# Cross-attention and a quantised FFN in one program: weights quantised in the loop, first rows fed through while the attention drains

## The chip, the cores and the metric

One Trainium2 chip, one core of it. The time is the device time of one execution in microseconds (us), and less is better. The core has engines that run side by side, each through its own list of instructions: TensorE (PE; its weight loads are shown apart as PEld), VectorE (DVE), ScalarE (ACT), GpSimd (POOL) and SyncE (SP), which here issues all DMAs. They wait for each other by semaphores alone.

## What is computed

The kernel takes `x` (8 batches x 112 rows x 512) and a context (8 x 375 x 256), and computes a cross-attention of 16 heads of 128 columns with RMS norms on q and k, and behind it an FFN of 512 -> 2048 -> 512 whose matmuls work on values rounded to 8 bits. Cut to what matters:

```
def rmsnorm(x, g): return x * rsqrt(mean(square(x), -1) + 1e-5) * g
h = layernorm(x)
q, k, v = h @ Wq, ctx @ Wk, ctx @ Wv            # 16 heads of 128
attn = softmax(rmsnorm(q, gq) @ rmsnorm(k, gk).T / sqrt(128))
x = x + (attn @ v) @ Wo
# FFN
X1 = layernorm(x)
X1_q = round(X1 * (127 / max|X1| of the row));    W1_q = round(W1 * (127 / max|W1|))
X2 = gelu(X1_q @ W1_q.T * (sX1 * sW1 / 127**2) + B1)
X2_q = round(X2 * (127 / max|X2| of the row));    W2_q = round(W2 * (127 / max|W2|))
x = x + X2_q @ W2_q.T * (sX2 * sW2 / 127**2) + B2
```

One scale holds for a whole weight matrix, so it is known only when all of that matrix has been read.

## The kernel before

**Attention.** Every operand of a matmul is kept as two float32r tensors, a high part and the rest (`_hi`, `_lo`), and each product is three matmuls. The work is cut into NI = 16 iterations `it`: 8 groups of two heads for the first four batches, then the same 8 for the last four. Each iteration has NB = 4 batch steps b; t = 4 * it + b numbers them from 0 to 63. A batch step computes K (`k_projection`), its squares and their sums (`k_norm`), scores, maximum, exponential, the transposes of the probabilities and their product with the context (`prob_ctx`). It is spread over several steps: in step t an engine works on t, t-1, t-2 and t-3 at a time. Once per iteration come `q_projection` (24 matmuls), `q_norms`, `v_projection` and `o_projection`, which adds into Y two iterations later. Each engine's list for a step is written by hand in its `step(it, b)`, and `run` unrolls some iterations and loops over the others. GpSimd splits weights, contexts and the squares into parts (`split`), ScalarE makes the high parts and VectorE the low ones.

**Weights of the FFN.** 16 chunks of 1024 columns (`wst`) are read through the loop, one in each iteration, and VectorE takes their maxima (`chunk_max`, L926). After the last, in iteration 15, GpSimd takes the maximum over the partitions (`partition_all_reduce`, L379) and VectorE the factors (L919). Then W1 is read a second time, 4 MB at once (L247 ff.), rounded by ScalarE (`round_weights`, L1152) and converted to bf16 in four pieces by GpSimd, ScalarE (2) and VectorE (`finish_w1`). W2 is treated likewise in the next block.

**The FFN** is a second block of its own behind the attention's. The 896 rows are NT = 7 tiles of 128. Tiles 0 to 2 (`EARLY_ROWS`) are rows of the first half only, so their sums are complete early. They are normed and quantised while the attention drains; 3 to 6 (`LATE_ROWS`) as one group behind it. Per tile: `up` (16 matmuls of 512 columns into four PSUM banks), `dequantise` (L1356, four pieces), gelu, `hidden_scale` (row maximum, L1362), `hidden_magic` (ScalarE adds a constant that rounds), `hidden_round` (L1370), `turn` (16 transposes, copied by ScalarE), `down` (16 matmuls), `scale_output` (L1375) and `finish` (L1380). The loop in the block of each engine sets their order, one tile ahead of the other.

Of the kernel before, what the change touches and what calls it, by code (L numbers as in the profile page):

```python
# [29 lines left out]
F32R = mybir.dt.float32r  # L30
BF16 = mybir.dt.bfloat16
# [44 lines left out]
def run(eng, step, peeled=()):  # L76

    step(0, 0)  # L80
# [45 lines left out]
def attention(nc, ctx, x, ctx_t, ctx_r, wq, wk, wv, wo, gq, gk, w12, shared):  # L126
    Y = shared.Y
# [9 lines left out]
    ident, eps = shared.ident, shared.eps  # L137
# [38 lines left out]
    spare = sps + [kps[0]]  # L176
    rows = shared.rows
# [990 lines left out]
def ffn(nc, ctx, w12, b1, b2, out, shared):  # L1168
# [64 lines left out]
    def _(pe):  # L1233
# [52 lines left out]
        for j in range(NT + 1):  # L1286
# [282 lines left out]
```

## Time and profile before

| | us |
|---|---|
| median of 3 runs (lowest, highest) | 821.6 (821.39, 823.34) |
| the profiled execution, own time | 818.36 |
| its span, first to last instruction | 816.6 |
| TensorE busy, share | 730.8, 89% |
| VectorE / ScalarE / GpSimd busy | 519.4 / 528.5 / 456.9 |
| mean granted TensorE clock | 0.958 |

Line numbers are those of the kernel before. Busy is time in which an engine had an instruction under way. Where several instructions overlap in the pipeline, the difference of two starts tells what one costs in a row. The granted clock is 1.00 at 2.4 GHz and 0.50 at 1.2 GHz. In brackets behind a row stands how long the engine had been idle before it, and what ended that.

### The profile page before, as it was taken

The page shows a single profiled execution, that of the slowest core. Times are in us where ns is not written, and L with a number is a line of the kernel's source. Part 1 is how long each engine was busy: PE and PEld are TensorE (multiplying, and loading weights), DVE is VectorE, ACT ScalarE, POOL GpSimd, SP SyncE. Part 2 cuts the span into 40 slices and gives each one's busy share as a digit, 9 for nine tenths or more (in the row PEclk, how much of TensorE's full clock was granted, in tenths as well). Part 3 has the DMA queues.
Part 4 walks back from the last instruction along what each step waited for, and adds up shares of the span by engine and source line. Part 5 has one row for each costly group of instructions (what it writes and reads, how often), then busy time and mean ns, then how long its engine had stood idle before and what let it go on. Part 6 is the DMA issues. An engine that isn't in the chain of part 4 may idle for free. (4 is left out here: it accounts for less than half of the span.)

```text
span 816.6 us, 15878 instructions
## 1 busy us (share of the span) xinstructions
PE 730.8 (89%) x4573; PEld 674.8 (83%) x4580; DVE 519.4 (64%) x1180; ACT 528.5 (65%) x1171; POOL 456.9 (56%) x477
## 2 busy tenths in 40 slices
PE   1839899999999999999899999999999998673995
PEld 1738899999999999899899999999999998551442
DVE  7555556565656565876455656565656565579894
ACT  2436677767767767675666777767777764548773
POOL 2554867666676766577675767666676742603000
PEclk9979999999999999999999999999999999687998
DMA  5331021111112111313202021111111153034001
GB/s 166 87 85 53 22 101 59 46 65 39 64 39 64 39 64 58 111 41 108 68 16 97 28 75 50 53 64 39 64 39 64 39 200 136 1 109 161 13 27 51
DMA packets 34859, 55.24 MB, mean 68 GB/s; under 512 B 2264, under 2 KB 23696, under 8 KB 34704
## 3 DMA queue, kind: packets, MB, share of 16 engines
q1 hardware_dynamic: 34832, 54.92, 20.0%
q8 instruction: 12, 0.20, 0.1%
q14 instruction: 15, 0.12, 0.0%
HBM read 53.08 MB, written 1.84 MB: 67 GB/s over the span
## 5 line engine op out<-in xcount | busy, mean ns | idle before, releaser
L428 PE MATMUL kps<-CTXT,WK 128*128 128x376 f32 x768 | 150.5, 338 | 2.6 <-POOL WK L292 1.7
L428 PEld LDWEIGHTS kps<-CTXT,WK 128*128 128x128 f32 x768 | 136.6, 191 | 6.1 <-issue 2.5
L292 POOL TENSOR_TENSOR KSQ_lo<-ksq,KSQ_hi 128x376 fp32r<-128x376 f32 x128 | 130.0, 1016 | 10.7
L290 POOL TENSOR_SCALAR KSQ_hi<-ksq 128x376 fp32r<-128x376 f32 x128 | 66.4, 519 | 114.2 <-ACT ksq L685 114.2
L949 DVE CUSTOM_DVE_ANT_0 prob<-sps,kr 112x375 f32<-112x375 f32 x128 | 68.7, 546 | 93.5 <-ACT kr L702 68.9
L697 ACT ACTIVATE kr<-kps,eps 112x376 f32<-112x376 f32 x128 | 73.6, 575 | 80.7 <-PE kps L449 80.4
L470 PE MATMUL cps<-PT_hi,CTX_hi 125*128 125x224 f32 x384 | 109.2, 284 | 3.7 <-DVE PC_lo L981 3.7
L470 PE MATMUL cps<-PT_hi,CTX_lo 125*128 125x224 f32 x384 | 107.4, 280 | 0.0
L470 PE MATMUL cps<-PT_lo,CTX_hi 125*128 125x224 f32 x384 | 107.3, 279 | 0.0
L707 ACT ACTIVATE prob<-prob,small,rq 112x375 f32<-112x375 f32 x128 | 89.5, 699 | 11.0 <-DVE small L958 11.0
L938 DVE TENSOR_TENSOR K_lo<-kps,K_hi 128x376 fp32r<-128x376 f32 x128 | 68.1, 543 | 42.9 <-ACT K_hi L692 42.5
L975 DVE TENSOR_TENSOR PT_lo<-tps,PT_hi 125x336 fp32r<-125x336 f32 x128 | 64.2, 501 | 45.4 <-ACT PT_hi L716 45.4
L685 ACT ACTIVATE ksq<-kps 128x376 f32<-128x376 f32 x128 | 61.8, 483 | 42.4 <-PE kps L428 40.8
L413 PE MATMUL xps<-XT,WQ 128*128 (+1 forms) x384 | 83.6, 373 | 2.0 <-DVE XT L889 2.0
L413 PEld LDWEIGHTS xps<-XT,WQ 128*128 128x128 f32 x384 | 73.1, 191 | 9.3 <-DVE XT L889 2.4
L470 PEld LDWEIGHTS cps<-PT_hi,CTX_hi 125*128 125x128 f32 x384 | 75.2, 196 | 4.1 <-issue 2.1
L457 PE MATMUL tps<-ident,prob 112*125 112x112 f32 x384 | 63.9, 276 | 14.4 <-DVE prob L969 9.2
L470 PEld LDWEIGHTS cps<-PT_hi,CTX_lo 125*128 125x128 f32 x384 | 75.4, 196 | 0.0
L470 PEld LDWEIGHTS cps<-PT_lo,CTX_hi 125*128 125x128 f32 x384 | 75.3, 196 | 0.0
L457 PEld LDWEIGHTS tps<-ident,prob 112*125 112x125 f32 x384 | 60.0, 194 | 16.3 <-DVE prob L969 10.1
L716 ACT ACTIVATE PT_hi<-tps 125x336 fp32r<-125x336 f32 x128 | 57.3, 448 | 18.9 <-PE tps L457 18.9
L702 ACT ACTIVATE kr<-kr 112x376 f32<-112x376 f32 x128 | 64.7, 521 | 0.5
(162 smaller groups left out, 1782.6 us busy)
## 6 DMA issues: line engine op xcount, KB each, us to landing
raw_a<-in_wq SPq DMA_DIRECT2D x16, 512.0 KB, 4.6
wst<-in_w SPq DMA_DIRECT2D x16, 512.0 KB, 4.7
raw_a<-in_wo SPq DMA_DIRECT2D x16, 512.0 KB, 3.9
W<-in_w SPq DMA_DIRECT2D x16, 512.0 KB, 8.2
raw_b<-in_wk SPq DMA_DIRECT2D x16, 256.0 KB, 4.8
raw_b<-in_wv SPq DMA_DIRECT2D x16, 256.0 KB, 2.8
raw_ct<-in_ctx_t SPq DMA_DIRECT2D x8, 376.0 KB, 3.4
raw_c<-in_ctx_r SPq DMA_DIRECT2D x8, 375.0 KB
```

The costliest lines, as they stand in the source:

```text
L290: pool.tensor_scalar(hi, raw, 1.0, 0.0, ALU.mult, ALU.add).then_inc(sem_, 1)
L292: pool.tensor_tensor(lo, raw, hi.bitcast(F32), ALU.subtract).then_inc(sem_, 1)
L413: ins = pe.matmul(xps[h][:, 0:HT], WQ[st][:, k, h * DH:(h + 1) * DH], XT[mo][:, k, bass.ds(col, HT)], start=(n == 0), stop=(n == 3 * KT - 1))
L428: ins = pe.matmul(kps[h][:, 0:SK], WK[st][:, k, h * DH:(h + 1) * DH], CTXT[mo][:, b, k, :], start=(n == 0), stop=(n == 3 * CT - 1))
L457: ins = pe.transpose(tps[0:KP, c * SQ:(c + 1) * SQ], prob[s][0:SQ, h, c * KP:(c + 1) * KP], ident[0:SQ, 0:SQ])
L470: ins = pe.matmul(cps[:, cc * G * SQ:(cc + 1) * G * SQ], CTX[st][0:KP, b, c, cc * P:(cc + 1) * P], PT[s][mo][0:KP, c, :], start=(n == 0), ...
L697: act.activation(kr[0:SQ, h, :], kps[h][0:SQ, 0:SK], ACT.Ln, bias=eps[0:SQ, :], scale=1.0 / DH)\
L702: act.activation(kr[0:SQ, h, :], kr[0:SQ, h, :], ACT.Exp, scale=-0.5).then_inc(a_rk, 1)
L707: act.activation(prob[s][0:SQ, h, 0:SKV], prob[s][0:SQ, h, 0:SKV], ACT.Exp, scale=rq[0:SQ, h, b:b + 1], bias=small[s][0:SQ, 1, h:h + 1], a ...
L938: dve.tensor_tensor(K[s][1][:, h, :], kps[h][:, 0:SK], K[s][0][:, h, :].bitcast(F32), ALU.subtract)\
L949: dve.tensor_tensor_reduce(prob[s][0:SQ, h, 0:SKV], sps[h][0:SQ, 0:SKV], kr[0:SQ, h, 0:SKV], 1.0, -3.0e38, ALU.mult, ALU.max, small[s][0:S ...
L975: dve.tensor_tensor(PT[s][1][0:KP, :, h * SQ:(h + 1) * SQ], tps[0:KP, 0:KC * SQ].rearrange("p (c n) -> p c n", c=KC), PT[s][0][0:KP, :, h ...
```

## The change

Attention and FFN become one block, with one list for each engine:

- `PEELED` is (0, 1, 7, 8) on every engine; loops run over iterations 2 to 6 and 9 to 14. The steps behind `q_projection(15)` are written out one by one, in one list for each engine, and mix the attention's last 13 steps with the FFN.
- The maxima of all 16 chunks are taken in iterations 0 to 7, two in each (b = 2 and b = 3). GpSimd's all-reduce stands at the end of step (8, 0), the factors at the end of (8, 1).
- W1 is read again in iterations 7 to 14, one chunk at a time, rounded by ScalarE and converted by VectorE in b = 3 of 8 to 15. Its bf16 form lies where the first half's XT was.
- W2 comes through two staging buffers in the drain, eight chunks, all rounded by ScalarE and converted by VectorE. GpSimd converts no weights any more.
- The rows of the FFN are treated one by one. The inverse root starts from a guess made of integer operations and takes three Newton steps, all on VectorE; before, ScalarE gave the start and one step followed.
- `dequantise` takes two pieces of 1024 columns, h has three buffers and hq two. The final additions of tiles 0 to 5 are GpSimd's.

```
-PEELED = (NG - 1, NG)
+PEELED = (0, 1, NG - 1, NG)
+ROW_GROUPS = (EARLY_ROWS, range(3, 5), range(5, NT))
...
+        def ffn_weights(it, b, late):
+
+            if not late and b in (1, 3) and not (first_of(it, NG - 1) and b == 3):
+                n = 2 * it + (b + 1) // 2
+                wait(sp, v_wm, n)
+                sp.dma_start(wst[:, :], w12[n]).then_inc(d_wm, 16)
+            if first_of(it, NG - 1) and b == 3:
+                sp.wait_ge(v_wm, WCH)
+                sp.dma_start(wst[:, :], w12[0]).then_inc(d_w1, 16)
+            if late and b == 3:
+                sp.wait_ge(v_w1, it - (NG - 1))
+                sp.dma_start(wst[:, :], w12[it - (NG - 1)]).then_inc(d_w1, 16)
...
-            if first_of(it, NI - 1) and b == 3:
+            if first_of(it, NG) and b == 0:
                 for n in range(2):
                     pool.wait_ge(v_wred, n + 1)
-                    pool.partition_all_reduce(shared.wall[:, n:n + 1], wred[:, n:n + 1], P,
+                    pool.partition_all_reduce(wall[:, n:n + 1], wred[:, n:n + 1], P,
...
+        def convert_w1(it):
...
+            dve.wait_ge(a_w1, it - (NG - 1))
+            settle(dve, n_dve)
+            dve.tensor_scalar(W1q[:, bass.ds((it - NG) * 1024, 1024)], wst[:, :], MAGIC, 0.0, ALU.subtract, ALU.add)\
+               .then_inc(v_w1, 1)
...
-                if new:
-                    chunk_max(it)
+                if not late:
+                    chunk_max(2 * it + 0)
...
+                if not late:
+                    chunk_max(2 * it + 1)
+                if late:
+                    convert_w1(it)
                 if two:
                     normalise(t - 2, 1, 1)
...
+        def round_w1(it):
+
+            act.wait_ge(d_w1, 16 * (it - (NG - 1)))
+            if first_of(it, NG):
+                act.wait_ge(v_wsc, 1)
+            act.activation(wst[:, :], wst[:, :], ACT.Copy, bias=MAGIC, scale=wsc[:, 0:1]).then_inc(a_w1, 1)
...
+        def w2_chunk(n):
+            wait(sp, p_q, G * NI)
+            if n == 1:
+                sp.wait_ge(v_w1, WCH // 2)
+            wait(sp, v_w2, n - 1)
+            sp.dma_start(staging[n % 2][:, :], w12[WCH // 2 + n]).then_inc(d_w2[n % 2], 16)
...
+def first_root(dve, link, r, var):
+
+    bits = [r[:, n, :].bitcast(I32) for n in range(4)]
+    link(dve.tensor_scalar(r[:, 2, :], var, EPS, None, ALU.add))
+    link(dve.tensor_scalar(bits[1], bits[2], 1, None, ALU.logical_shift_right))
+    link(dve.tensor_scalar(bits[1], bits[1], -1, ROOT_GUESS, ALU.mult, ALU.add))
+    link(dve.tensor_scalar(r[:, 3, :], r[:, 2, :], -0.5, None, ALU.mult))
```

The end of VectorE's new list, in the names of the code:

```
+        hidden_scale(4)
+        hidden_scale(5)
+        dequantise(6, 0)
+        hidden_round(4)
+        dequantise(6, 1)
+        hidden_round(5)
+        scale_output(3)
+        hidden_scale(6)
+        hidden_round(6)
+        scale_output(4)
+        scale_output(5)
+        scale_output(6)
+        finish(6)
```

GpSimd before, at the end of iteration 15: `KSQ` are the squares of K, `wall` the all-reduce's output.

```order
L292 TENSOR_TENSOR WO_lo<-raw_a,WO_hi 128x1024
L290 TENSOR_SCALAR KSQ_hi<-ksq 128x376
L292 TENSOR_TENSOR KSQ_lo<-ksq,KSQ_hi 128x376
L290 TENSOR_SCALAR KSQ_hi<-ksq 128x376
L292 TENSOR_TENSOR KSQ_lo<-ksq,KSQ_hi 128x376
L379 ISA
L379 ISA wall<-wred 128x1 x2
L290 ISA
L290 TENSOR_SCALAR WV_hi<-raw_b 128x512
```

GpSimd now, in iteration 8 from the first `k_squares` on; `CTX` is the context of the second half.

```order
L405 TENSOR_SCALAR KSQ_68<-ksq 128x376
L407 TENSOR_TENSOR KSQ_69<-ksq,KSQ_68 128x376
L405 TENSOR_SCALAR CTX_hi<-raw_c 125x768
L407 TENSOR_TENSOR CTX_lo<-raw_c,CTX_hi 125x768
L487 ISA
L487 ISA wall<-wred 128x1 x2
L405 ISA
L405 TENSOR_SCALAR KSQ_68<-ksq 128x376
L407 TENSOR_TENSOR KSQ_69<-ksq,KSQ_68 128x376
L405 TENSOR_SCALAR WV_hi<-raw_b 128x512
```

The all-reduce has moved from behind the last squares to between two squares of iteration 8.

VectorE before, b = 3 in the loop, from the last maximum of the scores to the second K_lo:

```order
L949 ISA prob,small<-sps,kr 112x375
L949 ISA small 112x1
L958 SCALAR_TENSOR_TENSOR small<-small,rq 112x2
L969 TENSOR_SCALAR prob<-prob,small 112x375
L937 ISA
L938 TENSOR_TENSOR K_lo<-kps,K_hi 128x376
L975 TENSOR_TENSOR PT_lo<-tps,PT_hi 125x3x112
L937 REGISTER_ALU
L938 TENSOR_TENSOR K_lo<-kps,K_hi 128x376
```

The same place now, in the loop over iterations 2 to 6:

```order
L1451 ISA prob_71,small<-acc,kr 112x375
L1451 ISA small 112x1
L1460 SCALAR_TENSOR_TENSOR small<-small,rq 112x2
L1426 ISA
L1428 ISA
L1428 TENSOR_REDUCE wmax<-wst 128x1
L1471 TENSOR_SCALAR prob_72<-prob_72,small 112x375
L1439 ISA
L1440 TENSOR_TENSOR K_66<-acc,K_65 128x376
L1477 TENSOR_TENSOR PT_76<-tps,PT_75 125x3x112
L1439 REGISTER_ALU
L1440 TENSOR_TENSOR K_66<-acc,K_65 128x376
```

The reduction stands ahead of `normalise` and of both K_lo; `kps` and `sps` are now parts of `acc`.

TensorE before, from the last `o_projection` to the first `up`, across the end of the block:

```order
L519 MATMUL xps<-O_lo,WO_hi 128x448
L519 MATMUL xps<-O_hi,WO_lo 128x448
L1537 UNCONDITIONAL_BRANCH
L1232 UNCONDITIONAL_BRANCH
L1476 MATMUL yps<-ident,Y 128x128 x4
L1476 MATMUL acc<-ident,Y 128x128 x12
L1245 MATMUL tp<-f_identb,xq_early 128x128 x12
L1256 MATMUL acc<-W1q_56,xqT 128x512
```

TensorE now, from the last matmuls of the last `prob_ctx` on; L631 is `v_projection(15)`, L809 `up`, L780 a turn.

```order
L598 MATMUL cps<-PT_75,CTX_lo 128x224
L809 MATMUL acc<-W1q,xqT_83 128x512 x4
L780 MATMUL tps<-identb,xq_early 128x128 x4
L809 MATMUL acc<-W1q,xqT_83 128x512 x4
L631 MATMUL xps<-PC_77,WV_hi 128x448
...
L631 MATMUL xps<-PC_77,WV_lo 128x448
L809 MATMUL acc<-W1q,xqT_83 128x512 x8
L809 MATMUL acc<-W1q,xqT_84 128x512 x12
```

The first two tiles' `up` now stand ahead of the attention's last `v_projection` and `o_projection`.

## Rows read from the trace of the kernel before

**Rows 1.** The page, parts 1 and 2: busy us and share; TensorE's tenths by slice.

```profile
PE 730.8 (89%) x4573; PEld 674.8 (83%) x4580; DVE 519.4 (64%) x1180; ACT 528.5 (65%) x1171; POOL 456.9 (56%) x477
...
PE   1839899999999999999899999999999998673995
```

**Rows 2.** Stages: us, busy (count) by engine, granted clock, DMA share, GB/s.

```profile
482.90:522.50 39.60, 39.60 (x262) 38.55 (x261) 24.50 (x61) 28.25 (x70) 26.11 (x29) 1.00 0.16 53
...
649.60:680.00 30.40, 30.40 (x209) 29.81 (x209) 18.84 (x51) 21.16 (x53) 16.82 (x19) 1.00 0.42 152
680.00:690.00 10.00, 7.05 (x38) 6.39 (x37) 4.15 (x17) 4.43 (x11) 0.72 (x2) 0.83 0.60 222
690.00:726.90 36.90, 24.65 (x109) 21.55 (x107) 22.74 (x45) 17.35 (x19) 12.60 (x6) 0.77 0.00 1
726.90:760.00 33.10, 18.64 (x106) 11.90 (x108) 30.13 (x52) 24.45 (x26) 7.36 (x2) 0.74 0.45 167
760.00:800.40 40.40, 36.79 (x222) 18.49 (x224) 38.06 (x55) 28.18 (x30) 0.00 (x0) 1.00 0.07 27
...
800.00:817.00 17.00, 9.80 (x47) 4.38 (x48) 5.77 (x10) 4.07 (x5) 0.00 (x0) 0.86 0.12 46
```

**Rows 3.** Timeline of VectorE in the FFN: start, us, what, idle before.

```profile
776.42 2.72 DVE L1356 SCALAR_TENSOR_TENSOR h<-acc,row_amax,B 128x512 f32<-128x512 f32 x4
...
780.19 0.68 DVE L1380 TENSOR_TENSOR X<-X,y 128x512 f32<-128x512 f32 x1
...
784.63 2.72 DVE L1356 SCALAR_TENSOR_TENSOR h<-acc,row_amax,B 128x512 f32<-128x512 f32 x4
...
802.52 1.23 DVE L1370 TENSOR_SCALAR hq<-h 128x2048 bf16<-128x2048 f32 x1 [1.39 <-ACT h L1315]
```

**Rows 4.** Timelines of VectorE and TensorE: reduction, K_lo and its user, W1 conversion.

```profile
503.49 1.20 DVE L926 TENSOR_REDUCE wmax<-wst 128x1024 f32 x1
...
519.04 0.54 DVE L938 TENSOR_TENSOR K_lo<-kps,K_hi 128x376 fp32r<-128x376 f32 x1
...
520.49 0.34 PE L440 MATMUL sps<-K_hi,Q_hi 128*112 128x376 f32 x1
...
721.60 1.23 DVE L1164 TENSOR_SCALAR W1q<-W 128x2048 bf16<-128x2048 f32 x1 [0.40 <-ACT W1q L1162]
```

**Rows 5.** Timeline of GpSimd, 678 to 690: last squares and the all-reduces.

```profile
678.33 1.01 POOL L292 TENSOR_TENSOR KSQ_lo<-ksq,KSQ_hi 128x376 fp32r<-128x376 f32 x1
688.79 0.72 POOL L379 PARTITION_ALL_REDUCE wall<-wred  x2 [9.45 <-issue]
```

**Rows 6.** Line 1114, the maxima of each matrix: durations, first and last start.

```profile
L1114 DVE TENSOR_REDUCE wred<-wmax x2: 150/152/153, 666.7 to 666.8; 128x1 f32<-128x8 f32 x2
```

**Rows 7.** Timelines in iteration 8: GpSimd, VectorE, TensorE.

```profile
362.17 0.51 POOL L290 TENSOR_SCALAR KSQ_hi<-ksq 128x376 fp32r<-128x376 f32 x1
...
365.00 2.44 DVE L901 TENSOR_TENSOR CTXT<-raw_ct,CTXT 128x752 fp32r<-128x752 f32 x1
...
370.09 0.63 PE L449 MATMUL kps<-KSQ_hi,ones 128*112 128x376 f32 x1
```

**Rows 8.** Timeline of TensorE: restart, last `prob_ctx` matmul, the first `up` matmuls.

```profile
700.02 0.94 PE L457 MATMUL tps<-ident,prob 112*125 112x112 f32 x3 [5.07 <-DVE PT_lo L975]
...
710.90 0.41 PE L470 MATMUL cps<-PT_hi,CTX_lo 125*128 125x224 f32 x1
...
731.58 6.85 PE L1256 MATMUL acc<-W1q,xqT 128*128 128x512 bf16 x31 [0.47 <-ACT xqT L1301]
```

**Rows 9.** Timelines of GpSimd and VectorE, 702 to 710: conversion and the small steps.

```profile
702.40 7.13 POOL L1164 TENSOR_SCALAR W1q<-W 128x2048 bf16<-128x2048 f32 x1
...
706.93 2.62 DVE L1143 TENSOR_SCALAR row_rstd<-row_mv 128x3 f32<-128x3 f32 x1
709.59 0.17 DVE L1144 TENSOR_TENSOR row_rstd<-row_rstd 128x3 f32<-128x3 f32 x1
709.78 0.16 DVE L1145 TENSOR_TENSOR row_rstd<-row_rstd 128x3 f32<-128x3 f32 x1
```

More of the change, by code:

```diff
@@ L257, in step @@
+        def step(it, b, late):
             for half in range(2):
@@ L522, in o_projection, with step @@
             ins.then_inc(p_y, 1)
-        def step(it, b):
+        def step(it, b, late):
             t = it * NB + b
@@ new lines, in turn_into, with turn_x @@
+        def turn_into(n, rows, first):
+            wait(pe, a_turn, turn_before(n) + 1)
+            if n >= FIXED_TURNS and turn_bank(n):
+                pe.wait_ge(v_x1, NT)
+            tb = turns[turn_bank(n)][:, :].bitcast(BF16)
+            for k in range(4):
+                ins = pe.transpose(tb[:, k * P:(k + 1) * P], rows[:, (first + k) * P:(first + k + 1) * P], identb[:, :])
+            ins.then_inc(p_turn, 1)
+        def turn_x(j, probs_done=0):
+            wait(pe, v_ptlo, probs_done)
+            if j == 0:
+                pe.wait_ge(s_const, 4)
+            pe.wait_ge(v_xq, j + 1)
+            turn_into(turn("x", j), xq[j], 0)
@@ new lines, in down @@
+        def down(j):
+            pe.wait_ge(a_turn, turn("h", j, 3) + 1)
+            if j == 0:
+                pe.wait_ge(v_w2, WCH // 2)
+                pe.wait_ge(v_pclo, LAST_T)
+            wait(pe, v_y2, j)
+            for f in range(FT):
+                ins = pe.matmul(yps[:, :], hqT[j % 2][:, f, :], W2q[:, f * D:(f + 1) * D],
+                                start=(f == 0), stop=(f == FT - 1))
+            ins.then_inc(p_down, 1)
+        prob_ctx(14, 57, 1, 1)
+        q_norms(15)
@@ L1125, in step @@
[L1125 to L1143 removed]
+            if first_of(it, NG) and b == 0:
+                weight_max()
@@ new lines, in _ @@
+        moments(1)
+        convert_w2(0)
+        y_add(13, 2)
+        normalise(60, 0, 0)
+        convert_w2(1)
+        k_low(61, 1, 1)
+        y_add(13, 3)
+        k_low(62, 2, 0)
+        prob_low(60, 0, 0)
+        score_max(61, 1, 0)
+        normalise(60, 0, 1)
+        add_rows(2)
+        prob_ctx_low(59, 3)
+        score_max(61, 1, 1)
+        moments(2)
+        exponent_bias(15, 61, 1)
+        row_root(0)
+        convert_w2(2)
+        row_norm(0)
+        prob_low(60, 0, 1)
@@ new lines, in _ @@
+        y_add(14, 2)
+        y_add(14, 3)
+        row_quantise(1)
+        row_norm(2)
+        prob_ctx_low(63, 3)
+        row_factor(2)
+        dequantise(0, 0)
+        o_low(15, 0)
+        dequantise(0, 1)
+        convert_w2(6)
+        dequantise(1, 0)
+        row_quantise(2)
+        hidden_scale(0)
+        o_low(15, 1)
+        dequantise(1, 1)
+        convert_w2(7)
+        y_add(15, 0)
+        hidden_round(0)
+        y_add(15, 1)
+        hidden_scale(1)
+        y_add(15, 2)
@@ new lines, in _ @@
+        dequantise(2, 0)
+        y_add(15, 3)
+        hidden_round(1)
+        add_rows(3)
+        add_rows(4)
+        moments(3)
+        moments(4)
+        row_root(1)
+        row_norm(3)
+        dequantise(2, 1)
+        row_norm(4)
+        row_factor(3)
+        row_factor(4)
+        scale_output(0)
+        row_quantise(3)
+        add_rows(5)
+        add_rows(6)
+        moments(5)
+        hidden_scale(2)
+        moments(6)
+        row_quantise(4)
+        row_root(2)
+        hidden_round(2)
```

1203 lines of the change are left out of this document (716 added, 487 removed).

## The prediction, made before the change was timed

> **What bounds the kernel now.** I read the page first [rows 1]: TensorE is busy for 89% of the span, VectorE for 64%, and TensorE's tenths are 9 from slice 6 to slice 33 and fall to between 3 and 8 behind it. Then the table by stage [rows 2]. An iteration of the middle loop, 482.9 to 522.5, is 39.6 us long and TensorE is busy in all of it, so the loop is bound by TensorE. From 649.6 on (TensorE has just finished `q_projection` and the first `k_projection` of iteration 15, and stands where `run` ends in the changed kernel) the picture changes. TensorE is full until 680, then 7.05 of 10.00 us, 24.65 of 36.90 and 18.64 of 33.10, and from 760 it is full again while VectorE is busy for 38.06 of 40.40. So the last 816.6 - 649.6 = 167.0 us hold a hole of some 40 us between two dense parts. The attention drains, the FFN's inputs wait for DMAs and for a block boundary, and in the hole the granted clock falls to 0.77 and 0.74 of full speed. The chain of waits lies in the FFN from 726.9 on, and rows of the FFN follow at 8.2 us each (784.63 - 776.42), VectorE hardly ever free [rows 3].
>
> **The change, part by part.**
>
> *The absolute maxima, earlier.* 16 reductions of 1.20 us stay 16, but the second of each pair stands in b = 3 of iterations 0 to 7, ahead of `normalise`, `k_low` and the rest. At 519.04 K_lo starts, it ends at 519.58, and TensorE takes it at 520.49 [rows 4]: 0.9 us of slack. The inserted reduction takes about 1.1 us until the next starts, so TensorE loses some 0.3 us in each of about 7 iterations: 2 us. Bounds: 0 (hidden), and 8 (all 1.1 us each time).
>
> *Quantising W1 in iterations 8 to 15.* ScalarE gets one pass of 1024 columns and VectorE one conversion of 1024, half of the 1.23 us that 2048 took [rows 4], in b = 3. The conversion takes 0.6 of the 0.9 us slack and ScalarE has waited there for TensorE, so I take 0; the other end is 8 x 0.6 = 5, the earliest gain none, since TensorE is the bound already.
>
> *The all-reduce over partitions.* This is the part that speaks against the change. GpSimd ended its last square at 679.34, the maxima had been there since 666.8, and the two all-reduces were recorded only at 688.79, ending at 689.51: 10.2 us, of which 9.45 show as "issue" [rows 5, 6]. That was in the drain. Now it stands in iteration 8, behind the context split and ahead of `k_squares(8,0,1)`. The maxima come at about 367.6 there, behind CTXT_lo, which ends at 367.44 [rows 7]. GpSimd is then free at 377.8 and the squares (0.5 + 1.0, [rows 5, 7]) are ready at 379.3, while TensorE took them at 370.09: 9.2 us of stall, with TensorE, GpSimd's queue behind it (WV, further squares, contexts) and VectorE all late alike. A pause costs speed too: after 5.07 us of idle TensorE restarted at 700.02 at half clock [rows 8]. I add 0.8, to 10. Bounds 0 (the 9.45 us belonged to the full DMA queues of that place) and 13 (10.2 plus 3 us of work at half speed). The Trainium skill, GPSIMD Engine Reference, Instruction dispatch, says that the first call to freshly loaded code pays about 6 us, with no instruction of its own in the profile; by that the stall would be 5.7 instead of 9.2 us and the sum 3.5 us lower. The trace agrees on the kind, not on the size: 9.45.
>
> *The drain.* Up to the first `up(0,0)` TensorE's new list has 318 matmuls. Between 649.6 and 680.0 it did 209 in 30.40 us without a pause, 0.1455 us each [rows 2]; 318 x 0.1455 = 46.3 us. VectorE must do nearly as much beside it. It was busy for 18.84 + 4.15 + 22.74 = 45.7 us from 649.6 to 726.9. Off come work that now stands behind the point (four `y_add`, two `o_low`, one `xq`: 4.1), the W1 conversion of 1.2 and 2.5 of a VectorE instruction held up by GpSimd; on go seven conversions at 0.6 and the longer inverse root, 16 chained small steps instead of 5 at 0.2 [rows 9], together 6.4. That is 44.3. Two engines at 46.3 and 44.3 don't fit without gaps: I take 51, 4.7 above the larger; the ends are 47 and 61. The latter is how the kernel before does it, where the last `prob_ctx` ends at 711.2 (710.90 + 0.3, [rows 8]), 61.6 after 649.6. What is late next is the chain of batch step 63, from K to its transposes: it starts 28 us into the list and needs about 12, so it just fits.
>
> *The end of the FFN.* `dequantise(0,0)` follows 2.1 us later (two `up` of four matmuls at 0.22, [rows 8], and one turn). VectorE was busy for 30.13 + 38.06 + 5.77 = 74.0 us behind 726.9, seven rows and all. Changes: plus o_low, y_add, xq and two W2 conversions (5.3), minus three W2 conversions of 2048 (3.7), minus six final additions given to GpSimd (6 x 0.68 = 4.1, [rows 3]), plus two roots (5.4), minus 2.5 held up by GpSimd, minus 14 x 0.12 = 1.7 for dequantising a row in two pieces instead of four (2.72 us for four; that 0.12 of each 0.68 is a fixed part is my estimate, the ends are 0 and 3 in all). That gives 72.7. Of it 1.2 + 2.7 stand behind the start of the last `hidden_round`, so 68.8 must be done before it. To these come 2.4 for the last row's scaling: VectorE waits 1.39 us for it today, and the output step of some 0.7 that fills part of it now stands behind it; 0.3 for the gelu before. 2 more for lesser gaps. From the start of the last `hq` to the end was 816.6 - 802.52 = 14.1; that stays. Sum: 68.8 + 2.4 + 2 + 14.1 = 87.3.
>
> *Contention.* The tiny `rstd` step of VectorE at 706.93 took 2.62 us and ended as GpSimd's 7.13 us conversion did, at 709.5 [rows 9]. Such conversions leave GpSimd, which wins the 2 x 2.5 us above; the six additions come in, some 1.3 us each for 512 columns after 1.01 for 376 [rows 5]. The Trainium skill, GPSIMD Engine Reference, Specifications, has the SBUF interfaces of the two shared, for VectorE's 2-port modes and for its operations on two SBUF inputs: by it each addition could hold VectorE for 1.3 us, 8 in all. I keep 2 of that within the "lesser gaps", as only some of VectorE's steps here read SBUF in that mode; the other end is 8.
>
> *The sum.* The new tail is 51 + 2.1 + 87.3 = 140.4 against 167.0: 26.6 won. The loop loses 2 + 10 = 12. Net 14.6: a span of 802.0, 803.8 us for an execution that has the profiled one's 1.8 us around it. That execution (818.36) lay 3.2 below the median of the runs, 821.6; against the median I forecast 821.6 - 14.6 = 807.0.
>
> **The rivals.**
>
> *The drain stays a chain.* Its latency, not TensorE's work, sets the end: 61 instead of 51, so 817. For it: the holes from 681 to 727 end on PT_lo, PC_lo and O_hi, one on another. Against: the longest hole, 5.07 us [rows 8], stands behind two long passes of ScalarE over W1 that are now spread over the loop, and other work is put between the steps.
>
> *The all-reduce costs the loop nothing,* because its 9.45 us were due to queues that were full then: 797. For it: the DMA share was 0.60 from 680 to 690 [rows 2]. Against: nothing that GpSimd needed came through them.
>
> *The inserted steps in b = 3 hurt more.* If the waits there close up, 15 iterations lose about 0.7 us more: 817.
>
> *Slower: half clock in the drain.* TensorE runs at 1.2 instead of 2.4 GHz after each hole, as it did from 700 on. In the drain TensorE is the bound, so each microsecond of its work done at half speed costs one. At a granted clock of 0.70 the 46.3 us become 66, and the time 827. It decides from 14.6 us at half speed on, a clock of about 0.76, which is what 690 to 726.9 had (0.77). Against: that stretch had 12 us without work in 37, and the new list puts projections, turns and `up` there. In the FFN itself the same would cost little: 52 us of TensorE's work in 87.
>
> That the change doesn't do what it says would look like the first rival: `up(0,0)` no earlier.
>
> **How the numbers follow.** Forecast 0.50, chain 0.15, free all-reduce 0.15, steps in b = 3 0.08, half clock 0.12. A change under 0.3% (2.5 us) can't be told from none here. Free: all faster, 0.15. Forecast: 0.47 faster. Chain and steps at 817 lie 2 below the bound of 819.1: 0.14 faster, 0.06 the same, the rest slower. Half clock: 0.02 faster, 0.09 slower. Together 0.78, 0.09 and 0.13. The forecast's own range is 799 to 815 (drain 47 to 55, stall 6 to 12, gaps up to 6 more); to hold 8 in 10 it goes to 796, for most of the free all-reduce, and to 821, which leaves out half clock.
>
> **What would show it.** Right: iteration 8 about 10 us longer, with TensorE idle before a K norm and GpSimd on the all-reduce; the iterations 2 to 6 at 39.9 and 10 to 14 at 39.6; from the end of the loop to the first `up` 51 us, and from there to the end 89; VectorE busy for over 95% of the FFN part. Wrong: iterations of both halves longer than 40.5 us; a hole of several microseconds on TensorE between 660 and 710; `hidden_scale` waiting for ScalarE throughout; a granted clock under 0.8 in the drain.

## The result, and the profile after

Over 20 runs each the changed kernel took 825.0 us (821.91 to 828.9) and the kernel before 822.3 us: ratio 1.0037, 95% interval 1.0021 to 1.0053. It is slightly slower, where 807.0 was forecast, with 796 to 821 as the range. The profiled execution took 822.4 us, its span 820.2 us, 3.6 more than before.

All the comparisons below cut a trace at the same four places: the first `q_projection` matmul of iterations 2, 8, 9 and 15. They are found in the timeline of TensorE (matmuls `xps<-XT,WQ`). These are the windows between them, for the kernel before and then the changed one. Columns: stretch, its length, busy us (count) of TensorE, its weight load, VectorE, ScalarE and GpSimd, granted clock, DMA share, GB/s.

```profile
114.98:354.50 239.52, 238.23 (x1562) 231.29 (x1561) 150.50 (x371) 169.37 (x409) 157.16 (x169) 1.00 0.18 59
354.50:399.02 44.52, 41.59 (x262) 39.80 (x261) 30.16 (x68) 28.97 (x70) 33.34 (x33) 0.96 0.23 70
399.02:641.28 242.26, 239.59 (x1562) 232.70 (x1561) 147.13 (x365) 168.85 (x408) 160.51 (x172) 0.99 0.16 54
641.28:816.60 175.32, 135.66 (x772) 100.38 (x778) 124.08 (x234) 106.09 (x157) 41.90 (x34) 0.88 0.23 86
```

```profile
114.36:361.77 247.41, 238.93 (x1562) 231.43 (x1561) 161.36 (x377) 169.62 (x409) 157.47 (x169) 1.00 0.22 69
361.77:421.97 60.20, 43.01 (x261) 40.95 (x261) 30.81 (x70) 29.15 (x70) 33.63 (x35) 0.83 0.17 52
421.97:666.51 244.54, 241.00 (x1561) 232.91 (x1561) 145.91 (x366) 174.40 (x415) 161.86 (x172) 0.99 0.17 56
666.51:820.20 153.69, 128.53 (x779) 91.87 (x778) 123.47 (x266) 97.01 (x152) 35.11 (x35) 0.95 0.21 71
```

Against the forecast:

| part | forecast | measured |
|---|---|---|
| iterations 2 to 7 (second maximum) | +2 | +7.9 |
| iteration 8 (all-reduce) | +10 | +15.7 |
| iterations 9 to 14 (W1 conversion) | 0 | +2.3 |
| start | 0 | -0.6 |
| from iteration 15 to the end | -26.6 | -21.6 |
| sum | -14.6 | +3.6 |

The gain of the drain is there. The part up to iteration 15 gives it all back: 25.2 us lost, the start counted, where 12 were forecast.

**Iteration 8.** GpSimd's timeline, the answer to [rows 5]:

```profile
371.90 2.00 POOL L407 TENSOR_TENSOR CTX_lo<-raw_c,CTX_hi 125x768 fp32r<-125x768 f32 x1
381.87 0.72 POOL L487 PARTITION_ALL_REDUCE wall<-wred  x2 [7.96 <-issue]
389.61 0.49 POOL L405 TENSOR_SCALAR KSQ<-ksq 128x376 fp32r<-128x376 f32 x1 [7.03 <-issue]
390.19 0.97 POOL L407 TENSOR_TENSOR KSQ<-ksq,KSQ 128x376 fp32r<-128x376 f32 x1
```

The two all-reduces are recorded with 0.72 us. GpSimd stands 7.96 us before them and 7.03 us again behind them, before an ordinary operation. Each of the two waits begins with a pair of instructions of its own, which do not count as busy and which the timeline leaves out. They show when the trace is asked for the two lines (duration in ns, first and last start):

```profile
L487 POOLq MODIFY_POOL_CONFIG  x2: 12/12/12, 373.9 to 373.9; - x2
L405 POOLq MODIFY_POOL_CONFIG  x2: 83/83/83, 382.5 to 382.6; - x2
```

TensorE waits for that square of the keys and starts again at half clock, 0.50 from 391.31 to 395:

```profile
391.31 0.94 PE L576 MATMUL acc<-KSQ,ones 128*112 128x376 f32 x2 [13.74 <-POOL KSQ L407]
```

**Iterations 2 to 7.** VectorE's timeline in b = 3 of iteration 4, the answer to [rows 4]:

```profile
231.76 1.22 DVE L1428 TENSOR_REDUCE wmax<-wst 128x1024 f32 x1 [0.17 <-issue]
232.90 1.10 DVE L1471 TENSOR_SCALAR prob<-prob,small 112x375 f32<-112x375 f32 x1
233.92 0.54 DVE L1440 TENSOR_TENSOR K<-acc,K 128x376 fp32r<-128x376 f32 x1
```

```profile
234.51 0.59 PE L567 MATMUL acc<-K,Q_hi 128*112 128x376 f32 x2 [1.04 <-DVE K L1440]
```

Not only the 1.22 us of the reduction delays `k_low`: `normalise` behind it takes 1.10 us instead of 0.41, as it now falls together with GpSimd's split of the squares (232.20 to 233.78). Iterations 2 to 6 take 40.76 us each instead of 39.59; iteration 7 takes 43.6 instead of 41.6.

**The tail.** In this execution the first `up` starts 53.8 us after the place that the prediction counts from (forecast 51), `dequantise(0,0)` 3.5 later (forecast 2.1), and the end 88.1 after that (forecast 87.3). The window up to the first `up`, in which TensorE is busy for 92%:

```profile
674.80:728.64 53.84, 49.54 (x322) 46.38 (x320) 43.58 (x116) 38.42 (x80) 21.27 (x23) 0.94 0.39 132
```

### The profile page after: what moved, and what is told of

Its sections match the earlier page's. It is cut to its first block, busy times and chain, and to the rows that moved or that the text cites. A ratio compares the mean times of both kernels' runs of the same rounds, so it can differ in the third digit from the quotient of the medians.

```text
span 820.2 us, 15720 instructions
## 1 busy us (share of the span) xinstructions
PE 730.9 (89%) x4580; PEld 670.5 (82%) x4580; DVE 530.9 (65%) x1226; ACT 525.8 (64%) x1174; POOL 453.3 (55%) x481
## 4 chain that ended last, share of the span: by engine, by line
PE 68%; DVE 14%; issue 8%; DMA 3%; POOL 3%; ACT 3%; DVEq 0%; SPq 0%; ACTq 0%; POOLq 0%
PE acc L555 12%; PE cps L598 11%; PE xps L540 9%; PE xps L651 9%; PE acc L567 8%; PE acc L576 6%; PE tps L585 5%; PE xps L631 2%; PE xps L613 2%; DMA raw_ct<-in_ctx_t 2%; PE cps L820 2%; DVE hmax L1695 1%; DVE prob L1451 1%; PE acc L809 1%; DVE prob L1471 1%
## 5 line engine op out<-in xcount | busy, mean ns | idle before, releaser
L555 PE MATMUL acc<-CTXT,WK 128*128 128x376 f32 x768 | 153.2, 342 | 3.1 <-ACT kr L1026 1.6
L555 PEld LDWEIGHTS acc<-CTXT,WK 128*128 128x128 f32 x768 | 138.8, 194 | 6.9 <-ACT kr L1026 2.2
L1026 ACT ACTIVATE kr<-acc,eps 112x376 f32<-112x376 f32 x128 | 73.7, 576 | 108.8 <-PE acc L576 108.7
L598 PE MATMUL cps<-PT,CTX_hi 125*128 125x224 f32 x768 | 135.9, 278 | 3.6 <-DVE PT L1477 3.2
L407 POOL TENSOR_TENSOR KSQ<-ksq,KSQ 128x376 fp32r<-128x376 f32 x128 | 130.0, 1016 | 10.7
L1451 DVE CUSTOM_DVE_ANT_0 prob<-acc,kr 112x375 f32<-112x375 f32 x128 | 68.8, 546 | 86.3 <-ACT kr L1031 59.0
L598 PEld LDWEIGHTS cps<-PT,CTX_hi 125*128 125x128 f32 x768 | 120.0, 193 | 4.5 <-DVE PT L1477 3.6
L598 PE MATMUL cps<-PT,CTX_lo 125*128 125x224 f32 x384 | 105.8, 276 | 0.0
L1477 DVE TENSOR_TENSOR PT<-tps,PT 125x336 fp32r<-125x336 f32 x128 | 64.3, 502 | 53.8 <-ACT PT L1045 53.5
L576 PE MATMUL acc<-KSQ,ones 128*112 128x376 f32 x256 | 72.0, 374 | 22.4 <-POOL KSQ L407 14.4
L540 PE MATMUL xps<-XT,WQ 128*128 128x448 f32 x384 | 82.9, 373 | 3.2 <-DVE XT L1373 3.2
L540 PEld LDWEIGHTS xps<-XT,WQ 128*128 128x128 f32 x384 | 73.8, 193 | 9.3 <-DVE XT L1373 3.6
L598 PEld LDWEIGHTS cps<-PT,CTX_lo 125*128 125x128 f32 x384 | 74.0, 193 | 0.0
L1045 ACT ACTIVATE PT<-tps 125x336 fp32r<-125x336 f32 x128 | 57.6, 450 | 18.2 <-PE tps L585 18.0
```

The source lines that it names most:

```text
L407: pool.tensor_tensor(lo, raw, hi.bitcast(F32), ALU.subtract).then_inc(sem_, 1)
L540: ins = pe.matmul(xps[h][:, 0:HT], WQ[st][:, k, h * DH:(h + 1) * DH], XT[:, bass.ds(col + mo * XW + k * HT, HT)], start=(n == 0), stop=(n ...
L555: ins = pe.matmul(kps[h][:, 0:SK], WK[st][:, k, h * DH:(h + 1) * DH], CTXT[mo][:, b, k, :], start=(n == 0), stop=(n == 3 * CT - 1))
L576: ins = pe.matmul(kps[h][0:SQ, 0:SK], ones[:, 0:SQ], KSQ[mo][:, h, :], start=(mo == 0), stop=(mo == 1))
L598: ins = pe.matmul(cps[:, cc * G * SQ:(cc + 1) * G * SQ], CTX[st][0:KP, b, c, cc * P:(cc + 1) * P], PT[s][mo][0:KP, c, :], start=(n == 0), ...
L1026: act.activation(kr[0:SQ, h, :], kps[h][0:SQ, 0:SK], ACT.Ln, bias=eps[0:SQ, :], scale=1.0 / DH)\
```

## The experiments

Each was timed in five rounds against the kernel before. In the traces, a stretch of unchanged code repeats within 0.1 us in the plain iterations. It varies in the start (iteration 2 begins at 113 to 118 us), in iterations 7 to 9 (up to 3 us each) and in the tail: nine traces with the changed kernel's roots have 152.4 to 155.8 us behind the start of iteration 15. The FFN part within the tail, from the first `dequantise` to the last `hidden_round`, repeats far better: 72.4 us in the changed kernel, e5 and e6, equal to 0.02. Differences below what a part varies by are not claimed.

### What the all-reduce costs where it stands, and where it stood

**e9_plain_copy** and **e10_before_plain_copy** put the same edit into the changed kernel and the kernel before:

```diff
-                    pool.partition_all_reduce(wall[:, n:n + 1], wred[:, n:n + 1], P,
-                                              bass.bass_isa.ReduceOp.max).then_inc(g_wall, 1)
+                    pool.tensor_copy(wall[:, n:n + 1], wred[:, n:n + 1]).then_inc(g_wall, 1)
```

> The changed kernel with GpSimd's two all-reduces replaced by two plain copies of 128 values at the same place (what it leaves out: the maximum over partitions; each keeps its own). This takes the whole price of the all-reduce out of the changed kernel and nothing else. Theory A (both waits, 7.96 and 7.03 us, belong to it): iteration 8 takes 44.5 to 45.5 instead of 60.2 us, the end comes 15 us earlier, near 809. Rival: if only the first wait does, 8 us and 817.

> The kernel before with the same edit, in its drain (what it leaves out: the maximum over partitions). It says what the all-reduce cost where it stood. Theory A: GpSimd loses both waits (9.45 and 7.28 us), but had little queued behind them (WV and WO for the last projections), and VectorE stood 3.21 us for it: 3 to 6 us less, 817. With e9 this gives the price of moving it: about 10 us. Rival (it was on the path there with its whole length): 10 to 16 us less, so that moving it cost nothing.

e9: 809.0 us, ratio 0.9841 (0.9804 to 0.9877); against the changed kernel 0.9841 / 1.0037 = 0.9805, 16 us. Iteration 8 takes 45.05 us, half a microsecond more than before the change (44.52):

```profile
362.98:408.03 45.05, 41.57 (x262) 39.94 (x262) 30.82 (x70) 29.16 (x70) 33.40 (x35) 0.96 0.23 69
```

```profile
375.96 0.49 POOL L487 COPY wall<-wred 128x1 f32<-128x1 f32 x2 [0.94 <-DVE wred L1404]
376.42 0.50 POOL L405 TENSOR_SCALAR KSQ<-ksq 128x376 fp32r<-128x376 f32 x1
377.00 0.99 POOL L407 TENSOR_TENSOR KSQ<-ksq,KSQ 128x376 fp32r<-128x376 f32 x1
```

Both waits are gone, with them the `MODIFY_POOL_CONFIG` pairs at 373.9 and 382.5, and 60.20 - 45.05 = 15.15 us. Theory A holds; the rival with one wait does not.

e10: 823.0 us, ratio 1.0008 (0.9989 to 1.0028). The expectation of 3 to 6 us was wrong: in the drain of the kernel before the all-reduce cost nothing, at most 0.9 us. Its GpSimd, with the copy:

```profile
682.72 0.30 POOL L379 COPY wall<-wred 128x1 f32<-128x1 f32 x2
689.43 0.62 POOL L290 TENSOR_SCALAR WV_hi<-raw_b 128x512 fp32r<-128x512 f32 x1 [6.41 <-issue]
```

The wait of 6.41 us is for a DMA: `raw_b`, issued at 680.88, took 8.4 us to land. In the kernel before, the same DMA was issued at 677.45 and had landed by 685.9, so it explains none of the 7.28 us ahead of `WV_hi` there. They begin with a `MODIFY_POOL_CONFIG` pair (689.45), as in the changed kernel. Nobody needed WV so early (the kernel before):

```profile
696.78 0.61 POOL L290 TENSOR_SCALAR WV_hi<-raw_b 128x512 fp32r<-128x512 f32 x1 [7.28 <-issue]
712.66 0.71 PE L501 MATMUL xps<-PC_hi,WV_hi 128*128 128x448 f32 x1 [1.34 <-issue]
```

TensorE's hole of 5.07 us [rows 8] stays as it was, and VectorE's 3.21 us for the all-reduce became 3.13 us for TensorE. (The profiled execution of e10 has a tail 4 us longer than the profile of before; the 12 timed runs do not bear that out as a cost of the copy.) So moving the all-reduce cost its whole price of 15 us.

### Is the wait paid once, or at each change?

**e2_split**: the second all-reduce one step later, with GpSimd's ordinary splits between the two.

```diff
-            if first_of(it, NG) and b == 0:
-                for n in range(2):
-                    pool.wait_ge(v_wred, n + 1)
-                    pool.partition_all_reduce(wall[:, n:n + 1], wred[:, n:n + 1], P,
-                                              bass.bass_isa.ReduceOp.max).then_inc(g_wall, 1)
+            if first_of(it, NG) and b in (0, 1):
+                pool.wait_ge(v_wred, b + 1)
+                pool.partition_all_reduce(wall[:, b:b + 1], wred[:, b:b + 1], P,
+                                          bass.bass_isa.ReduceOp.max).then_inc(g_wall, 1)
```

(`weight_factors` moves from b = 1 to b = 2 with it.)

> The changed kernel, the two all-reduces in two steps of iteration 8 (b = 0 and b = 1), with GpSimd's ordinary splits between them. Theory A (each change to the all-reduce's code and each change back costs, every time): GpSimd shows four waits of 7 to 8 us, iterations 8 and 9 together get some 15 us longer and the total is 837. Rival (the wait is paid at the first call alone, once for the all-reduce's code and once for what stood there first): two waits as before, total within 2 us of 825.

842.8 us, ratio 1.0266 (1.0229 to 1.0304), where 837 was expected. GpSimd:

```profile
385.83 0.38 POOL L486 PARTITION_ALL_REDUCE wall<-wred  x1 [9.38 <-issue]
393.83 0.49 POOL L405 TENSOR_SCALAR KSQ<-ksq 128x376 fp32r<-128x376 f32 x1 [7.63 <-issue]
...
415.26 0.38 POOL L486 PARTITION_ALL_REDUCE wall<-wred  x1 [8.06 <-issue]
422.61 1.03 POOL L405 TENSOR_SCALAR WQ<-raw_a 128x1024 fp32r<-128x1024 f32 x1 [6.97 <-issue]
```

Four waits, each with its `MODIFY_POOL_CONFIG` pair at its start, and iteration 8 takes 78.78 us, 18.6 more. The wait belongs to each change between the all-reduce and ordinary operations, in both directions, not to the first call. Two all-reduces in a row share one. What GpSimd does in it the trace does not show.

### The maxima and the conversion in b = 3

**e3_moves**: both go ahead of `score_max(t - 1, 2, 1)`, where VectorE waits 3.25 us in any case.

```diff
                     y_add(it - 2, 3)
+                if not late:
+                    chunk_max(2 * it + 1)
+                if late:
+                    convert_w1(it)
                 if one:
                     score_max(t - 1, 2, 1)
                     exponent_bias(it, t - 1, 2)
-                if not late:
-                    chunk_max(2 * it + 1)
-                if late:
-                    convert_w1(it)
```

> The changed kernel, with the maximum (iterations 0 to 7) and the conversion of W1 (8 to 15) in b = 3 moved ahead of score_max(2, 1), into the 3.2 us in which VectorE waits for ScalarE's K norm. Theory A (they delay K_lo of step 3, for which TensorE waits): iterations 2 to 7 fall from 40.7 to 39.5, iterations 10 to 14 from 39.9 to 39.6, in all 7 to 9 us less than the changed kernel, about 816. Rival (the 1.2 us are due to something else that came with the change: the DMA of 512 KB twice per iteration, contention for SBUF): periods stay at 40.7, 825.

816.7 us, ratio 0.9942 (0.9921 to 0.9964), 7.8 us less than the changed kernel. Iterations 2 to 6 take 39.5 us each instead of 40.8, iterations 10 to 14 39.6 instead of 39.9: the kernel before's values. VectorE:

```profile
227.81 1.21 DVE L1428 TENSOR_REDUCE wmax<-wst 128x1024 f32 x1
231.14 0.55 DVE L1451 CUSTOM_DVE_ANT_0 prob<-acc,kr 112x375 f32<-112x375 f32 x1 [2.12 <-ACT kr L1031]
...
231.81 0.41 DVE L1471 TENSOR_SCALAR prob<-prob,small 112x375 f32<-112x375 f32 x1
```

The doubled DMAs and their traffic are still there, so the rival falls for these iterations. Iteration 7, which also splits contexts, stays long (44.8 us; 41.6 before the change, 43.6 after). So e3 takes back 5.2 of the 7.9 us lost up to iteration 8. Iterations 7 to 9 together took 130.4 us before the change. In e5 and the five kernels built on it, which have neither the all-reduce nor the steps in their old place, they take 133.6 to 136.1. Why these 3 us and more stay was not tried.

### The maximum over partitions without GpSimd

**e1_bounce**: two DMAs by way of DRAM, and a reduction on VectorE. **e4_both** is e1 and e3 together. **e5_late_factors** is e4 with VectorE's use of the result one step later (the second diff).

```diff
+            if first_of(it, NG) and b == 1:
+                sp.wait_ge(v_wred, 2)
+                sp.dma_start(maxima.rearrange("n p -> p n"), wred[:, :],
+                             allow_slow_non_contiguous=True).then_inc(d_m, 16)
+                sp.wait_ge(d_m, 16)
+                sp.dma_start(wback[:, :, :], maxima.rearrange("(a n) p -> a n p", a=1).to_broadcast([P, 2, P]))\
+                  .then_inc(d_m, 16)
...
-            dve.wait_ge(g_wall, 2)
+            dve.wait_ge(d_m, 32)
+            link(dve.tensor_reduce(wall[:, :], wback[:, :, :], AX.X, ALU.max))
```

```diff
-            if first_of(it, NG) and b == 1:
+            if first_of(it, NG) and b == 2:
                 weight_factors()
```

> The changed kernel, with the maxima over partitions taken without GpSimd: the 2 x 128 values go to DRAM and come back to all partitions by two DMAs, and VectorE reduces them. Theory A (GpSimd waits about 8 us before the all-reduce and 7 us behind it, because it changes between two sets of code, and TensorE stands for both): iteration 8 falls from 60.2 us to 44.5 (as iteration 8 of the kernel before), so 15.7 less and about 807 us at the profile, 809 against the median. Rival B (the time belongs to iteration 8 itself: context splits, DMAs, straight-line code that the engines run for the first time): iteration 8 stays at 55 us or more, the total above 819. Rival C (only the first wait of 8 us belongs to the all-reduce): 8 less, 817.

> Both edits of the first and third run in one kernel. If the two costs are independent, their gains add up: 15.7 + 8 = 24 less than the changed kernel, about 801, with the tail of 145.4 us behind the loop unchanged. If the tail has a chain of its own that depends on how the loop ends, it is not: above 806.

> The kernel of e4_both, with weight_factors at the end of step (8, 2) instead of (8, 1) on VectorE. In e4_both VectorE stood there until the two DMAs had landed (11.25 + 2.86 us, the first behind the 512 KB of raw_a), and TensorE stood for 8.4 us. Theory A: now nothing waits for the maxima; iteration 8 falls from 55.3 to about 45, total 802 to 804. Rival (iteration 8 has a second cost of its own, which the waits hid: the context splits or the copies): it stays above 50, total above 808.

| kernel | us | ratio to before | iteration 8 | iteration 15 to end |
|---|---|---|---|---|
| changed | 825.0 | 1.0037 (1.0021 to 1.0053) | 60.20 | 153.7 |
| e1 | 819.8 | 0.9987 (0.9959 to 1.0014) | 55.28 | 153.5 |
| e4 | 812.2 | 0.9893 (0.9854 to 0.9933) | 55.3 | 155.8 |
| e5 | 802.9 | 0.9769 (0.9732 to 0.9806) | 45.48 | 153.5 |

e1 gained 5 us where 15.7 were expected. By its own expectation this reads as rival B, a second cost of iteration 8. The trace shows that it was not: one in-order wait had taken the place of another. The small DMA was issued right behind the 512 KB of `raw_a` and took 11.2 us to land, 0.2 us after `raw_a` did; the second took 2.9. VectorE stood in `weight_factors` with all its work behind it. (Whether the place in the queue or the DMA's own pieces of 4 bytes made it slow was not isolated.) VectorE, then TensorE, in e1:

```profile
390.79 0.42 DVE L1416 TENSOR_REDUCE wall<-wback 128x2 f32<-128x256 f32 x1 [8.88 <-DMA wback<-maxima]
```

```profile
394.74 0.97 PE L581 MATMUL acc<-KSQ,ones 128*112 128x376 f32 x2 [8.43 <-DVE K L1446]
```

e4 missed its 801 us for the same reason, with iteration 8 at 55.3; against e1 it gained 7.6 us, nearly e3's 8. With the wait one step later (e5) the values are there before anyone asks: 9.3 us less than e4, as expected, and 22 less than the changed kernel. Iteration 8 agrees with e9's 45.05, so the rival of a second cost in it falls.

### The tail: which engine sets its pace?

**e6_drain_order** is e5 with the root of the first rows behind the steps that TensorE waits for. **e8_shorter_roots** is e6 with two Newton steps instead of three (behind the dots).

```diff
         exponent_bias(15, 61, 1)
-        row_root(0)
+        prob_low(60, 0, 1)
         convert_w2(2)
-        row_norm(0)
-        prob_low(60, 0, 1)
-        score_max(62, 2, 0)
         k_low(62, 2, 1)
         o_low(14, 0)
+        score_max(62, 2, 0)
         k_low(63, 3, 0)
+        row_root(0)
...
-            for _ in range(3):
+            for _ in range(2):
                 newton(dve, link, rstd[:, :, r])
```

> e5_late_factors, and in the drain VectorE's prob_low(60, 0, 1), a conversion of W2, two k_low, o_low and score_max(62, 2, 0) stand ahead of the inverse root of the first rows, whose 16 chained small steps took 4.9 us there; ScalarE's row_magic(0) and VectorE's row_quantise(0) move back with it. Theory (TensorE's hole of 3.22 us and the clock of 0.54 to 0.80 behind it come from prob_low waiting behind these steps, and TensorE bounds the drain): the hole goes, the tail is 3 to 5 us shorter, total about 799. Rival (VectorE, not TensorE, sets the pace of the drain and of the FFN behind it, so an order alone moves nothing): within 1 us of e5_late_factors.

> e6_drain_order with two Newton steps instead of three in each of the three inverse roots of rows (what it leaves out: the third step, which changes the result by a few millionths). 12 small steps of VectorE at 0.2 us fewer, 2.4 us of its time. If VectorE sets the end, 2 us faster than e6_drain_order; if the roots stand where VectorE would wait anyway, no change.

e6: 802.1 us, ratio 0.9769 (0.9733 to 0.9805): no difference from e5, as its rival said (799 was expected). The hole of 3.22 us went from `prob_ctx` and came back as one of 3.06 us before a later `prob_transposes`, whose `normalise` now stands behind the root. The clock of the drain rose from 0.94 to 0.97 and the first `dequantise` came 1.1 us earlier, which is within what the tail varies by.

e8: 797.6 us, ratio 0.9721 (0.9683 to 0.9759). The tail is 149.69 us against 153.00 in e6, and below all nine of 152.4 to 155.8. 12 small steps, 2.4 us of VectorE's time, were left out. Eight of them stand between the first `dequantise` and the last `hidden_round`, and this part fell from 72.4 to 70.8 us: their 1.6 us, fully. The rest of the 3.3 lies before and behind it, where the same code varies by 0.5 to 1.4 us. From `dequantise(1, 0)` to the last `hidden_scale` VectorE (third busy time of the row) has 62.66 us of work in 64.67, 97%:

```profile
711.87:776.54 64.67, 52.06 (x312) 28.52 (x311) 62.66 (x118) 43.06 (x46) 5.55 (x4) 0.96 0.09 33
```

**e7_finish_on_dve** is e5 with the six additions back on VectorE, **e11_round_on_act** e8 with three roundings of hidden rows on ScalarE, **e12_root_on_act** e8 with the first root begun on ScalarE. Their diffs in this order; in e7 the six calls go from GpSimd's list, in e11 the three from VectorE's.

```diff
         scale_output(0)
+        finish(0)
...
         scale_output(5)
+        finish(5)
```

```diff
+            act.activation(hq[j % 2][:, :], h[j % 3][:, :], ACT.Copy, bias=-MAGIC).then_inc(v_hq, 1)
...
         hidden_magic(0)
+        hidden_round(0)
```

```diff
+            act.activation(rstd[:, 0, js], mv[:, js, 1], ACT.Ln, bias=eps[:, :]).then_inc(s_act, 1)
+            act.wait_ge(s_act, 5)
+            act.activation(rstd[:, 1, js], rstd[:, 0, js], ACT.Exp, scale=-0.5).then_inc(s_act, 1)
...
+            minus_half(dve, link, rstd[:, :, r], mv[:, r, 1])
+            newton(dve, link, rstd[:, :, r])
```

> e5_late_factors with the final additions of rows 0 to 5 back on VectorE (0.68 us each, in the kernel before) instead of GpSimd (1.26 to 1.5 us each). By the working of the prediction (VectorE bounds the FFN part, six additions are 4.1 us, GpSimd costs at most 2 by contention): 2 to 4 us slower than e5_late_factors. Rival (GpSimd's additions hold VectorE through the shared access to SBUF for as long as they last, 1.3 us each): 0 to 4 us faster.

> e8_shorter_roots with the rounding of the hidden rows 0 to 2 to bf16 (hidden_round, 1.22 us each on VectorE) on ScalarE, where it will take some 2 us each. If VectorE alone sets the pace of the FFN part (no idle time from 711.9 to 776.5 in e8_shorter_roots), 3 x 1.15 = 3.4 us less than it, about 794. If the chain from gelu over the scale to the turns sets it, no change or 1 to 2 us more.

> e8_shorter_roots with the inverse root of the first rows begun on ScalarE (a logarithm and an exponential, as the kernel before does it) and one Newton step on VectorE: 5 chained small steps instead of 12 in the drain, 1.4 us of VectorE's time, and about 1 us more where GpSimd's splits hold those steps. If VectorE's time bounds the drain as it bounds the FFN part, the first dequantise comes 1 to 2 us earlier and the total is 796. If the drain is bound by TensorE (46 us of work) and chains, no change against e8_shorter_roots.

e7: 805.7 us, ratio 0.9815 (0.9776 to 0.9854); the intervals overlap, so timing alone does not decide. (The profiled execution of e7, 797.64 us, was the fastest of its eight; its lead of 7 us lies ahead of iteration 15.) In the trace the tail is the same, 153.56 against 153.48 (e5 first, then e7), with 4.2 us more of VectorE's work in it and 8.1 less of GpSimd's:

```profile
649.22:802.70 153.48, 129.65 (x779) 92.01 (x778) 123.55 (x266) 96.99 (x152) 35.40 (x35) 0.95 0.20 71
```

```profile
642.14:795.70 153.56, 129.02 (x779) 90.95 (x778) 127.77 (x272) 96.90 (x152) 27.30 (x29) 0.96 0.20 71
```

But the drain up to the first `dequantise` came out 1.3 us shorter in e7 with the same code, which hides a difference behind it. From the first `dequantise` to the last `hidden_round` e7 needs 74.8 us, e5 72.4; behind it e7 needs 14.5, e5 15.5. Four of the six additions, 2.7 us, stand in the first of these parts. So the transfer to GpSimd saves 2.4 us there, nearly all of the four, and seems to give back 1 at the end. What the latter is was not isolated.

e11: 801.2 us, ratio 0.9756 (0.9724 to 0.9788), and a tail of 153.36: slower than e8 by 3.7 in the trace. The rival was right, and even too mild (1 to 2 us more). The part from the first `dequantise` to the last `hidden_round` takes 73.8 us against 70.8. VectorE loses 3.0 us of work (117.82 against 120.84), but ScalarE's rounding takes 1.91 us (VectorE's took 1.22) and stands ahead of the next gelu, and VectorE then waits 2.35 us for that gelu and 3.1 for TensorE's transposes of Y:

```profile
724.04 2.29 DVE L1712 TENSOR_REDUCE hmax<-h 128x1 f32<-128x2048 f32 x1 [2.35 <-ACT h L1222]
```

So VectorE's time bounds the FFN part only as long as ScalarE's chain has its slack.

e12: 800.0 us, ratio 0.9719 (0.9685 to 0.9753), tail 149.46: no difference from e8 that can be told. The drain, where TensorE is busy for over 90%, gains nothing that can be told from 1.4 us less on VectorE: the first `dequantise` comes 0.7 us earlier, within what the drain varies by.

## Why the prediction was wrong

**The step that failed is "The all-reduce over partitions".** It put down 10 us, "9.2 stall + 0.8 clock", from one wait of 9.45 us. The trace of before had a second one, 7.28 us ahead of the next ordinary operation (`WV_hi`), and the prediction has no term for it. Counted from the start of iteration 8, the maxima came at 13.1 us, as forecast. The all-reduces then ended at 20.8, earlier than the forecast's 23.3, but the squares were ready only at 29.4 instead of 24.8: 2.5 us too much for the first wait, and 7.0 missing for the second. TensorE's hole was 13.74 us, and it came back at half clock. Measured as the price of the all-reduce: 15.15 us in the profile, 16 in the timed runs (e9). The upper bound of 13 was too low for the same reason. What the all-reduce had cost in its old place is no term of the forecast, whose tail was added up anew; e10 shows that it was nothing, since nobody needed what was queued behind it. The Trainium skill, GPSIMD Engine Reference, Instruction dispatch, which the prediction cited for about 6 us at the first call to freshly loaded code, has the kind of cost right. By it the stall would have been smaller still. The runs show a larger one, paid at each change (e2) and on the way back as well.

**"The absolute maxima, earlier"**: mechanism right, size wrong, and as large a miss as the first: 2 us forecast, 7.9 measured (the bound was 8). In iterations 2 to 6 it is 0.3 us forecast, 1.2 measured each. The slack of 0.9 us was read rightly, but the reduction comes with 0.17 of wait, and with 0.7 for `normalise`, pushed under GpSimd's split: 1.2 + 0.17 + 0.7 - 0.9 = 1.2. e3 took it away. I had costed the inserted instruction and not what it pushes its neighbours into. Iteration 7 lost 2.0 us, which e3 did not give back; their cause stays open.

**Quantising W1 in iterations 8 to 15**: 0 forecast, 2.3 measured in iterations 9 to 14, within its bound of 5. e3 removed it in iterations 10 to 14 (39.6 again). Taken together, the steps in b = 3 cost 10.2 us where 2 were forecast. That is most of what the rival "the inserted steps in b = 3 hurt more" had, which got a chance of 0.08.

**The drain**: 51 forecast, 53.8 measured; mechanism right. TensorE is 92% busy there, part of it at a clock of 0.94. The rival "the drain stays a chain" (61) did not happen, nor did half clock throughout it. The hole in it looked like a cause and was none (e6). The first `dequantise` followed 3.5 us later, not 2.1.

**The end of the FFN**: 87.3 forecast, 88.1 measured. Two small misses partly cancelled, and that is luck. From the first `dequantise` to the last `hidden_round` it took 72.4 us where 73.2 were added up (68.8 + 2.4 + 2; the "0.3 for the gelu" is not in that sum, and the 0.4 us from 800.0 to 800.4 are in two of the added rows). From there to the end it took 15.7, not 14.1. VectorE was busy for 97% of it as said, 63.99 of 66.27 us in the changed kernel:

```profile
736.20:802.47 66.27, 50.74 (x312) 28.11 (x311) 63.99 (x126) 43.06 (x46) 5.54 (x4) 0.97 0.09 32
```

In sum: the stall was 5.7 us short, the maxima 5.9, the conversion 2.3, the tail 5.0, and the start gave 0.6; these 18.2 us are the way from -14.6 to +3.6. All four misses went the same way, so their sum left the range, although only the stall left its own bounds. Without the waits of the all-reduce the changed kernel takes 809.0 us (e9), and with the maxima and the conversion moved as well and the result awaited late 802.9 (e5). The fastest version is e8: 797.6 us, ratio 0.9721 to the kernel before.

## What to carry to other kernels

- Before moving a step, price it at the place where it goes, not where it stands. Count every wait around it in the trace, before and behind, and ask separately what it costs in the old place. Here the old place hid 17 us of GpSimd's standing entirely. In the new one TensorE lost 13.7 of the 15.
- A wait that is taken off one engine's queue appears on another's unless its user is moved late as well (e1 against e5).
- An instruction put into slack costs its length less the slack, plus what it pushes the next ones into. Look for the engine's longest wait in the step and put it right ahead of that (e3).
- An operation that comes with a change of GpSimd's configuration has a wait on either side. Look for the `MODIFY_POOL_CONFIG` entries of its line before pricing it.

## What the runs showed of the hardware

- GpSimd's `partition_all_reduce` was recorded with 0.36 us. Each change to it left GpSimd idle for 8.0 to 9.4 us (before, changed kernel, e2), and each change back for 7.0 to 7.6. Nothing counts as busy in these waits; a `MODIFY_POOL_CONFIG` pair stands at the start of each. The kernels with the copy have no such pair but the one that every kernel has in its first 1.4 us. Two all-reduces in a row paid once.
- VectorE's `TENSOR_SCALAR` on SBUF took longer while GpSimd worked: 0.41 us (e3) became 1.10 beside a split of squares. In the drain of the changed kernel 0.54 became 2.46, and it ended 0.3 us after GpSimd's `WO_lo` (727.84 + 2.41):

```profile
728.08 2.46 DVE L1662 TENSOR_SCALAR xn_early<-X_early,mv,rstd 128x512 f32<-128x512 f32 x1
```

- A DMA of 1 KB in pieces of 4 bytes, issued right behind one of 512 KB, took 11.2 us to land (e1), 0.2 us after that one; in the other seven kernels that have it, it took 9.7 to 11.3. Which of the two made it slow was not isolated.
- After its 13.74 idle us TensorE came back at 1.2 GHz: in the changed kernel the six matmuls of 448 columns from 392.05 on start 0.37 us apart, at full clock 0.20.
